# A graph transformer layer on one core: the third chunk's first mix layer in the middle part, key sums with their own signal, and another order of the second chunk's gathers

## What is computed

```python
xn = layernorm(x)
# graph: alpha of edge e from the two ends of the edge, rows gathered by index
alpha = softmax(leaky_relu(alpha_l[src] + alpha_r[dst]))
x1 = x + sum_h alpha[n, h] * xt[dst[n], h]        # broadcast over the heads
# mix: linear attention over all 6250 rows at once
q, k, v = split(xn @ w_qkv + b_qkv);  k, v = ln(k), ln(v)
kv = einsum("hnd,hne->hde", k, v) / N
ret = einsum("hnd,hde->hne", q, kv) + xn
x1 = x1 + gelu(ret @ w1 + b1) @ w2 + b2 + xn
# experts: three layers each, weighed by a router
w = softmax(layernorm(x1) @ Wr + br)
y = sum_e w[:, e] * (relu(bn(relu(bn(z @ W1[e])) @ W2[e])) @ Wo[e] + bo[e])
out = x1 + y
```

## Time and profile before

| | |
|---|---|
| median of 3 runs | 1066.76 us (1066.09 to 1066.95) |
| profiled execution, its own time | 1066.64 us |
| its span | 1064.8 us |
| PE busy | 1056.3 us (99%) |
| PE weight loads busy | 901.3 us (85%) |
| DVE busy | 776.0 us (73%) |
| ACT busy | 728.4 us (68%) |
| POOL busy | 282.6 us (27%) |
| chain that ended last | PE 96%, DVE 2%, issue 1% |

### The profile page before, as it was taken

How to read it: one execution, slowest core, us unless ns; L and a number is a source line. 1 busy time by engine, 2 the same in 40 slices (tenths; PEclk the granted TensorE clock), 3 DMA queues, 4 the chain that set the end, 5 groups by cost and what they waited for, 6 DMA issues and landing times.

```text
span 1064.8 us, 16895 instructions
## 1 busy us (share of the span) xinstructions
PE 1056.3 (99%) x5316; PEld 901.3 (85%) x5316; DVE 776.0 (73%) x1642; ACT 728.4 (68%) x1265; POOL 282.6 (27%) x309
## 2 busy tenths in 40 slices
PE   9999999999999999999999999999999999999998
PEld 7989988888888888888888888888888888888898
DVE  7888766877686686776766877767768668676654
ACT  5777766676775766757757767667677576676765
POOL 4787864303022022130140321211402202110010
PEclk9999999999999999999999999999999999999999
DMA  6877763153244233441542343425425423340020
GB/s 189 260 239 253 235 198 101 42 133 105 61 104 115 86 70 109 113 114 40 140 115 80 81 109 99 98 67 126 120 50 116 115 84 65 94 110 15 12 71 15
DMA packets 229318, 115.78 MB, mean 109 GB/s; under 512 B 164433, under 2 KB 211797, under 8 KB 229229
## 3 DMA queue, kind: packets, MB, share of 16 engines
q1 hardware_dynamic: 224578, 107.35, 37.6%
q0 software_dynamic: 3968, 6.71, 2.5%
q10 hardware_dynamic: 683, 0.64, 0.2%
HBM read 77.07 MB, written 37.58 MB: 108 GB/s over the span
## 4 chain that ended last, share of the span: by engine, by line
PE 96%; DVE 2%; issue 1%; DMA 0%; ACT 0%; POOL 0%; DVEq 0%; POOLq 0%
PE bank L304 30%; PE bank L306 30%; PE bank L305 30%; PE bank L1158 2%; PE bank L1099 1%; PE bank L1346 1%; PE bank L1091 1%; PE bank L1364 1%; DMA alpha_l<-node_table,indices 0%; PE bank L1115 0%; DVE h_low L1421 0%; PE bank L1338 0%; DVE gathered L1626 0%; PE bank L1230 0%; PE bank L1108 0%
## 5 line engine op out<-in xcount | busy, mean ns | idle before, releaser
L820 ACT ACTIVATE h<-weight_stage 128x512 fp32r<-128x512 f32 (+2 forms) x206 | 116.4, 603 | 183.2 <-PE bank L306 116.4
L1421 DVE TENSOR_TENSOR h<-weight_stage,h 128x512 fp32r<-128x512 f32 (+2 forms) x206 | 127.0, 658 | 106.2 <-ACT h L820 105.6
L1421 DVE TENSOR_TENSOR h_low<-activated,h_high 128x512 fp32r<-128x512 f32 (+2 forms) x208 | 135.9, 665 | 76.3 <-ACT h_high L820 71.9
L971 ACT ACTIVATE activated<-bank,bn_cols 128x512 f32<-128x512 f32 (+2 forms) x208 | 154.9, 745 | 39.9 <-PE bank L306 37.9
L971 ACT ACTIVATE weight_stage<-bank,bn_cols 128x512 f32<-128x512 f32 (+2 forms) x208 | 150.1, 746 | 25.8 <-PE bank L306 25.0
L304 PE MATMUL bank<-h_high,ffn_w_high 128*128 128x512 f32 (+2 forms) x420 | 158.2, 377 | 1.1 <-DVE h_low L1421 1.0
L306 PE MATMUL bank<-h_high,ffn_w_low 128*128 128x512 f32 (+2 forms) x420 | 157.8, 376 | 0.0
L305 PE MATMUL bank<-h_low,ffn_w_high 128*128 128x512 f32 (+2 forms) x420 | 157.7, 376 | 0.0
L304 PE MATMUL bank<-xT_high,ffn_w_high 128*128 128x512 f32 (+2 forms) x416 | 156.9, 377 | 0.0
L305 PE MATMUL bank<-xT_low,ffn_w_high 128*128 128x512 f32 (+2 forms) x416 | 156.6, 376 | 0.0
L306 PE MATMUL bank<-xT_high,ffn_w_low 128*128 128x512 f32 (+2 forms) x416 | 156.6, 376 | 0.0
(11 more groups left out here) (248 smaller groups left out, 1997.9 us busy)
## 6 DMA issues: line engine op xcount, KB each, us to landing
expert_weight_rows<-expert_weights SPq DMA_DIRECT2D x44, 256.0 KB, 4.0
x_rows<-in_x SPq DMA_DIRECT2D x18, 512.0 KB, 4.8
x_turned<-xT_high SPq DMA_DIRECT2D x22, 256.0 KB, 3.6
x_turned<-xT_low SPq DMA_DIRECT2D x22, 256.0 KB, 4.6
x_rows<-accumulated SPq DMA_DIRECT2D x11, 512.0 KB
x_rows<-expert_weights SPq DMA_DIRECT2D x22, 256.0 KB, 5.6
accumulated<-x_rows SPq DMA_DIRECT2D x88, 64.0 KB, 2.1
out<-accumulated SPq DMA_DIRECT2D x88, 64.0 KB, 1.9
```

The costliest lines, as they stand in the source:

```text
L820: return nc.scalar.activation(dst, src, ACT.Copy)
L971: nc.scalar.activation(dst[:, h, 0:ch.rows], src[h][:, 0:ch.rows], ACT.Relu, bias=bnp[:, 1, layer, col:col + 1], scale=bnp[:, 0, layer, co ...
L1421: return V.tensor_tensor(dst, full, high.bitcast(fp32), ALU.subtract)
```

## The change

Three things are changed.

1. The key sums and the value sums are split into `key_sums` and `value_sums`. Those that need only older tiles come first; the key sums get a signal of their own, `m_key`, for which VectorE waits, and the value sums follow under `m_sum`. The two `w1m` matmuls come last, in place of `idle(5)`.
2. `mix1` of chunk 2 goes from step 2 of chunk 1's expert loop into the middle part, in place of `idle(9)`. It writes to the banks of the experts' first layer (`L1b`), so the first `L1` waits for its Gelus (`gelu`, 6). Its input is loaded into the second half of `h_high` and `h_low`, by SyncE behind chunk 1's rows; its Gelu output lies in `xb0` until step 2 of chunk 1, where VectorE splits it as before. The weight rows of experts 4 and 5 of chunk 1, which are loaded into the same place, are loaded after that: SyncE waits for `fmh`, 12. ScalarE's load of the exponential's table goes behind `x2_high(CHUNKS[0])`.
3. GpSimd issues the first gather pair of chunk 1 ahead of chunk 0's exponent, and the last two pairs behind the norm of chunk 0 and its messages (`gmsg`), where they waited for `f2lo` and `h1`.

The core of the diff:

```diff
+
+        def mixed_first(ch):
+
+            return L2b if ch.c == 1 else L1b if ch.c == 2 else Fb
...
         def gel_of(ch, h):
+            if ch.c == 2:
+                return xb0[:, h, :]
...
             def load_turned(ch):
 
                 need(sp, xst(ch), turned_stored(ch))
-                if ch.c != 1:
+                if ch.c == 2:
+                    need(sp, s["kv"], NTILES)
+                    need(sp, s["xt"], NTILES)
+                elif ch.c != 1:
                     need(sp, s["fm2"], ch.b0)
-                for i, part in enumerate((h2h, h2l) if ch.c == 1 else (xmh, xml)):
+                home = (h2h, h2l) if ch.c == 1 else (h1h[:, 1, :, :], h1l[:, 1, :, :]) if ch.c == 2 else (xmh, xml)
+                for i, part in enumerate(home):
                     sp.dma_start(part[:, :, 0:ch.rows].bitcast(fp32),
-                                 xt_d[ch.c, i, :, :, ch.xc:ch.xc + ch.rows]).then_inc(s["xmB"] if ch.c == 1 else s["xm"], 16)
+                                 xt_d[ch.c, i, :, :, ch.xc:ch.xc + ch.rows]).then_inc((s["xm"], s["xmB"], s["xmC"])[ch.c] if ch.c < 3 else s["xm"], 16)
...
             need(sp, s_gath[0], gathered(CHUNKS[0]))
             load_rows(CHUNKS[1])
+            load_turned(CHUNKS[2])
...
                 if ch.c + 2 < NC:
+                    if ch.c == 1:
+                        need(sp, s["fmh"], 12)
+                        load_weights(ch, range(4, 6))
                     load_rows(CHUNKS[ch.c + 2])
                     load_idx(CHUNKS[ch.c + 2])
-                    load_turned(CHUNKS[ch.c + 2])
+                    if ch.c > 0:
+                        load_turned(CHUNKS[ch.c + 2])
...
                     load_weight_cols(ch.next())
-                    load_weights(ch.next(), range(2, NE - 1))
+                    load_weights(ch.next(), (2, 3, 6) if ch.c == 0 else range(2, NE - 1))
...
             gather(CHUNKS[0], range(CHUNKS[0].nt))
             blocks(CHUNKS[1])
+            pool.wait_ge(s["m_sum"], 1)
+            gather(CHUNKS[1], range(0, 1))
             first_exp(CHUNKS[0])
-            pool.wait_ge(s["m_sum"], 1)
-            gather(CHUNKS[1], range(0, 2))
+            gather(CHUNKS[1], range(1, 2))
             norm2(CHUNKS[0])
-            need(pool, s["f2lo"], KT)
-            gather(CHUNKS[1], range(2, 3))
-            need(pool, s["h1"], 1)
-            gather(CHUNKS[1], range(3, 4))
+            need(pool, s["gmsg"], 1)
+            gather(CHUNKS[1], range(2, 4))
...
-                    elif ch.c != 1:
-                        need(act, s["f2T"], KT * ch.c)
-                    if ch.c > 2:
                         need(act, s["fin"], 2 * (ch.c - 2))
-                    nc.scalar.activation(gel_of(ch, h)[:, 0:ch.rows], (L2b if ch.c == 1 else Fb)[h][:, 0:ch.rows], ACT.Gelu,
+                    elif ch.c == 2:
+                        need(act, s["fxn"], 1)
+                    nc.scalar.activation(gel_of(ch, h)[:, 0:ch.rows], mixed_first(ch)[h][:, 0:ch.rows], ACT.Gelu,
                                          bias=c1c[:, h:h + 1]).then_inc(s["gelu"], 1)
...
             gel_high(CHUNKS[1], range(0, 1))
             gelu(CHUNKS[1], range(1, 2))
             gel_high(CHUNKS[1], range(1, 2))
+            gelu(CHUNKS[2])
+            x2_high(CHUNKS[0])
             nc.scalar.activation(warm[:, :], epsc[:, 0:1], ACT.Exp)
-            x2_high(CHUNKS[0])
             relu1(CHUNKS[0], 0)
...
-                    if nxt is not None and e in FRONT and not (nxt.c == 1 and e in (0, 2)):
+                    if nxt is not None and e in FRONT and not (nxt.c == 1 and e in (0, 2)) and not (nxt.c == 2 and e == 2):
...
-            for k in range(KT):
-                need(pe, s["kvn"], NTILES - 1)
-                nc.tensor.matmul(KVb[2 + k][:, 0:D], ident[:, :], w1m[:, k, :], start=True, stop=False)
...
+            s_product(NTILES - 2, 1, TAIL)
+            key_sums(kvn[:, 1, :], TAIL, start=True)
             need(pe, s["xte"], NTILES)
+            value_sums(kvn[:, 1, :], TAIL, start=True)
             pe.wait_ge(s["ksum"], NTILES - 1)
-            kv_sums(kvsum, P, start=True)
-            s_product(NTILES - 2, 1, TAIL)
-            kv_sums(kvn[:, 1, :], TAIL)
+            key_sums(kvsum, P)
             s_product(NTILES - 1, 0, TAIL, final=True)
-            kv_sums(kvn[:, 0, :], TAIL, stop=True).then_inc(s["m_sum"], 1)
-            idle(5)
+            key_sums(kvn[:, 0, :], TAIL, stop=True).then_inc(s["m_key"], 1)
+            value_sums(kvsum, P)
+            value_sums(kvn[:, 0, :], TAIL, stop=True).then_inc(s["m_sum"], 1)
+            for k in range(KT):
+                nc.tensor.matmul(KVb[2 + k][:, 0:D], ident[:, :], w1m[:, k, :], start=True, stop=False)
             pe.wait_ge(s["m_kv"], 2)
...
+                if ch.c == 0 and e == 0:
+                    need(pe, s["gelu"], 6)
...
+                dst = mixed_first(ch)
                 if ch.c == 1:
                     need(pe, s["xmB"], 32)
-                    dst, hi, lo = L2b, h2h, h2l
+                    hi, lo = h2h, h2l
+                elif ch.c == 2:
+                    need(pe, s["xmC"], 32)
+                    hi, lo = h1h[:, 1, :, :], h1l[:, 1, :, :]
                 else:
                     need(pe, s["flg"], ch.c)
-                    need(pe, s["xm"], 32 * max(ch.c, 1))
-                    dst, hi, lo = Fb, xmh, xml
+                    need(pe, s["xm"], 32 * max(ch.c - 1, 1))
+                    hi, lo = xmh, xml
...
             mix1(CHUNKS[1], range(1, 2))
-            idle(9)
+            mix1(CHUNKS[2])
             mix2(CHUNKS[1], range(0, 1))
...
-                    elif nxt is not None and e in FRONT and not (ch.c == 0 and e in (2, 3)):
+                    elif nxt is not None and e in FRONT and not (ch.c == 0 and e in (2, 3)) and not (ch.c == 1 and e == 2):
                         FRONT[e](nxt)
...
                     need(dve, s["gelu"], 2 * ch.c + h + 1)
                     need(dve, s["fm1"], 2 * ch.c + 2)
+                    need(dve, s["fm2"], ch.b0)
                     copy(hmh[:, h, 0:R], gel_of(ch, h)[:, 0:R]).then_inc(s["fmh"], 1)
...
-            dve.wait_ge(s["m_sum"], 1)
+            dve.wait_ge(s["m_key"], 1)
             md.step(V.scalar_tensor_tensor(t1, Ksum, bvc[:, :], t1, ALU.mult, ALU.add))
```

9 lines of the change are left out of this document (5 added, 4 removed).

## The result

The changed kernel takes 1060.99 us (median of 6 runs, 1060.79 to 1063.24), beside 1066.56 us (median of 6, 1066.09 to 1068.12) for the kernel before, run with it. The ratio is 0.995, 95% interval 0.994 to 0.996: 5.6 us less. The forecast was 1061.6, with a range from 1060.4 to 1063.8.

The account below looks back on a forecast made before the run. TensorE was taken as full in the expert loop, a dependency chain as setting the middle, plus one 1.03 us stop in chunk 0. Terms -1.1 - 1.5 - 2.77 + 0.3 = -5.07 from 1066.64 gave 1061.6 us, range 1060.4 to 1063.8.

Parts of the forecast that it names:

- Middle: From last table tile to first expert: key sums first and the mix layer for nine fillers start the expert loop 1.1 us earlier.
- TensorE just waits for the last normalised tile: Middle part: the last product could start at 154.37, but VectorE finishes its tile at 154.41.
- Chunk 1, the layer gone: Chunk 1's expert loop: twelve matmuls leave a full TensorE queue, -2.77 us.
- Chunk 0: Chunk 0's expert loop: gathers issued earlier remove VectorE's wait for the last one, -1.5 us, ends -1.2 and -1.8.
- VectorE gets 1.84, so at most that much: Chunk 0: TensorE gets at least 1.19 us back, up to 1.84 if later short stalls go too.
- What is late next there: nothing that the trace shows by name: Chunk 0: once the gather wait is gone, the trace names no next late item; no size given.
- The added wait: Chunk 1: SyncE stands until VectorE splits chunk 2's Gelu output, delaying chunk 3's indices; +0.3 us, ends 0 and 4.2.
- The slack is used up to the last tenth: Chunk 1: expert four's split is ready at 263.75, TensorE wants it at 263.82; nothing lost if indices land as before.
- A (indices late): Chunk 1: chunk 3's indices land late behind the weights, 1 to 4.2 us more, 1062.3 to 1065.5; chance 0.15.
- B (no gain in chunk 0): Chunk 0's expert loop: busy VectorE holds TensorE elsewhere, so the 1.5 us are not gained, 1063.1; chance 0.06.
- C (turned input late): Middle: the turned input for chunk 2's mix layer arrives late, 2 us more, 1063.6; chance 0.04.
- D (the clock): Middle, up to the expert loop: without fourteen fillers the clock falls to half rate, 12 us more, 1073.6; chance 0.02.

Follow-up runs that it names:

- part 3 alone: Only the new order of GpSimd's chunk 1 gathers, put into the kernel before: 1064.54 us, ratio 0.9978 to 0.9996.
- parts 1 and 2: Changed kernel with GpSimd's chunk 1 gathers back in the old order: 1061.71 us, ratio 0.9940 to 0.9965.
- kernels with delays: Changed kernel with one or two small waited-for DMAs on SyncE's queue ahead of chunk 3's rows and indices: 1064.56 and 1066.64 us.
- kernels without fillers: Kernel before without its five and nine filler matmuls, 1068.95 us, or without the nine alone, 1067.28 us.
- part 1 alone: Only the split key and value sums, with the weight-bank pair for five fillers, put into the kernel before: 1065.25 us, ratio 0.9978 to 0.9996.
- no fillers: Kernel before without its fillers of five and of nine matmuls, nothing in their place: 1068.95 us, ratio 1.0020.
- second ones out: Kernel before without the nine fillers between the two mix layers, the five kept: 1067.28 us, ratio 1.0010.
- one delay: Changed kernel with one scratch-row copy, waited for, on SyncE's queue between chunk 1's weight rows and chunk 3's rows and indices: 1064.56 us, ratio 0.9978.
- two delays: Changed kernel with two small DMAs, each waited for, on SyncE's queue between experts 4 and 5's weight loads and chunk 3's rows: 1066.64 us, ratio 1.0004.

## Why the prediction was right

**Middle, -1.1 forecast, -1.01 measured.** Right in its mechanism: VectorE's last pair moved by 1.02 instead of 1.19. The chain behind it was right too, ScalarE's value scalars as the new bound and the layer in the fillers' place. "TensorE just waits for the last normalised tile" held: that tile was ready at 154.25 + 0.69 = 154.94, its product started at 154.99. The term that was mis-sized is what follows it. From the product's start to ScalarE's it took 156.96 - 154.99 = 1.97 us, where I had 156.34 - 154.48 = 1.86, and from the scalars' end to their reader 157.67 - 157.55 = 0.12, where I had 0.05: together 0.18, where 0.17 are missing. The other mis-sized term was the room for the turned input, put at "over 6 us" and a cost of 0. The room was there, but the load needs nearly all of it: 6.25 us from issue to landing. The 0 held with 0.44 us to spare, which the prediction did not know.

**Chunk 1, the layer gone, -2.77 forecast, -2.77 measured** between the bias matmuls and the next expert. A full engine gives back what is taken out, one for one.

**Chunk 0, -1.5 forecast with ends -1.2 and -1.8, -1.97 measured, outside both ends.** Two steps of it failed. The upper end was "VectorE gets 1.84, so at most that much": TensorE got 2.30 back before the new pause, and 1.97 net. Which work on the other engines gave the excess over 1.84 is not shown. And the cause was half seen: the new order of the gathers is enough for the gain (-2.02 with part 3 alone), but not needed for it, since parts 1 and 2 without it give -1.96. The gather was late for the 4.2 us that it took to land beside 1 MB of loads, as much as for its place in GpSimd's queue. I carried that 4.2 into the new order as if it belonged to the gather; in the changed kernel, without the loads, it was 3.07. That the forecast of this stage came near although it left out what part 2 does there is partly luck. "What is late next there: nothing that the trace shows by name" was wrong as well: chunk 1's norm was next, at 0.44 us.

**The added wait, +0.3 forecast, +0.04 measured** (`L1` to `L3` of expert four, 24.66 before and 24.70 after). "The slack is used up to the last tenth" was too dark by 1.1 us. The indices did land later, 4.91 instead of 4.23, but their load was issued 0.7 earlier than I had it, 246.0 in chunk 1's old times (243.55 plus the 2.46 between the marks at 238.70 and 236.24) instead of 246.7, and so they were used at 250.92, where I had 250.9: two errors that cancelled, by luck. The 1.1 us come from two terms that were smaller than the rows that I took: the rescaling of the indices 0.19 instead of 0.68, the norm 0.28 + 1.04 instead of 0.28 + 1.54.

**Rivals.** A (indices late) did not come: they took 0.7 us longer to their use, inside the slack; the kernels with delays show that past the slack its price is real, and higher than A had it because of the clock. The order rule of the Trainium skill (DMA: Bandwidth & Descriptors, "Queues, rings and completion order"), by which the sum would have ended at 1062.3 or more, is not clearly borne out by the indices: from issue to use they took 4.9 with the weights just ahead, and with a delay between 4.3 in one kernel and 5.2 in the other, where the weights had landed before the indices were issued. The small copies fit it better, which landed 0.18 us after the weights ahead of them. No run here separates order from shared engines. B (no gain in chunk 0) fell. C (turned input late) did not come, but was near: the loads went out at 161.66 and 162.14, landed at 167.03 and 168.39, and the layer started at 168.83. D (the clock) did not come with the change, clock 1.00 in every stretch; but its mechanism is real, as the kernels without fillers show. The rule of the Trainium skill that an idle TensorE drops to the lower clock (TensorE: Matmul & The Clock Gate, "Part 1: The HAM clock gate") agrees with the gaps of 1.77 and 2.6 us. Pauses of 0.44 and 1.03 us left the clock at 1.00, and the fall near 10 us in three profiles came without any pause before it, which idleness alone does not explain. D's 12 us were far too much: the falls in the middle and in chunk 1 cost 1.3 to 1.8 us each.

The sum, -5.07, and the stages, -5.70, differ by the 0.47 that chunk 0 gave more, the 0.26 that the wait took less, and 0.09 in the middle the other way. The first stage gave 0.52 of it back in the profiled execution of after.

## What to carry to other kernels

When a wait ends with a DMA, look at what else was issued on the DMA engines in the microseconds before, and not only at where the transfer stands in its own queue: moving two large loads freed a gather that another part of the same change moved too, so the two gains did not add. Take fillers out only against work that fills the same gap. And price an added wait against its slack in microseconds, since past the slack the cost is the pause and a slow clock on top.

## What the runs showed of the hardware

- A gather of one tile (its second DMA, from the end of its issue) landed in at most 2.3 us with parts 1 and 2, in 3.1 in the changed kernel with a 512 KB load issued 1.1 us before it, in 4.2 behind 1 MB of loads (part 1 alone), and in 4.3 with that 1 MB issued just after it (part 3 alone).
- A load of 512 KB from memory, behind another of 512 KB and beside chunk 1's rows and gathers, took 6.25 us from issue to landing in the changed kernel, 5.59 with parts 1 and 2.
- TensorE's granted clock stayed 1.00 through pauses of 0.44 and 1.03 us. It fell to the lower level after idle times of 1.77 and 2.57 (no fillers), 2.55 (second ones out), 2.48 (one delay) and 3.10 us (two delays): after the 2.48 with the first matmuls, after the 3.10 only 1.6 us later (266.56 - 264.95), when matmuls went from 0.23 to 0.43. A fall cost 1.3 to 1.8 us besides the pause. In three of fourteen profiles it also fell near 10 us with no pause before it (0.66 from 9 to 14 us).
- A row of 1 KB copied from memory to memory by SyncE and waited for took 3.1 and 3.4 us right behind 512 KB of weight loads, and 1.8 issued after the first of them had landed.
- With part 3 alone, the runs with a mean granted clock of 0.998 took some 2.4 us more than those with 1.00 (median 1066.88 against 1064.48).
